# Sets of 128 edges for five destinations in a graph network's adjacency build

## The reference, cut to what matters

```python
x = x + attention(h, qW, kW, vW, src, dst)     # softmax over the edges of a source row
x = x + sage_pool(h, src, dst, ...)            # twice: segment_max(m[src], dst)
x = x + segment_sum((h @ G)[col] * w, row) + bG
x = x + sixteen rounds of  h = 0.9 * segment_sum(norm * h[row], col) + 0.1 * h0
```

## Time and profile before

| | us |
|---|---|
| median of 3 runs | 2932.34 (2927.5 to 2935.43) |
| span of the profiled execution | 2888.9 |
| PE, DVE, ACT, POOL busy | 2545.6, 1856.1, 1190.5, 1187.0 |
| front | 0 to 62.5 |
| build | 62.5 to 249 |
| attention and first dense layer | 249 to 703.6 |
| max pass 1, dense layer, max pass 2 | 703.6 to 1232, to 1311.3, to 1832 |
| third layer, propagation | 1832 to 2090, to 2888.9 |

### The profile page before, as it was taken

One profiled execution on the slowest core, in us unless ns is written; L12 is line 12 of the kernel. 1 busy time (PEld: TensorE's weight loads), 2 busy tenths in 40 slices (PEclk: granted clock), 3 DMA queues, 4 the chain that ended last, 5 costly groups with the idle time before them and its releaser, 6 DMA issues. The chain is left out here.

```text
span 2888.9 us, 69542 instructions
## 1 busy us (share of the span) xinstructions
PE 2545.6 (88%) x27756; PEld 1989.5 (69%) x27756; DVE 1856.1 (64%) x5232; ACT 1190.5 (41%) x2826; POOL 1187.0 (41%) x1385
## 2 busy tenths in 40 slices
PE   5888999995899889756999898368799999999999
PEld 3455777773566566534666565258699999999998
DVE  6997999996788778535887787251244444444444
ACT  4997888884344334423444344231121111111110
POOL 3003999993677667535777677410000000000000
PEclk8999999997999999878999999559999999999999
DMA  5103000004455445423555454529500000000000
GB/s 165 37 1 95 13 12 13 12 11 119 116 136 139 123 126 144 128 76 91 140 146 127 124 144 124 175 73 337 163 2 2 2 2 2 2 2 2 2 2 18
DMA packets 160514, 227.25 MB, mean 79 GB/s; under 512 B 59579, under 2 KB 126454, under 8 KB 159516
## 3 DMA queue, kind: packets, MB, share of 16 engines
q1 hardware_dynamic: 134184, 186.29, 20.8%
q0 software_dynamic: 22464, 35.14, 6.7%
q10 hardware_dynamic: 3540, 1.30, 0.2%
HBM read 122.95 MB, written 102.05 MB: 78 GB/s over the span
## 5 line engine op out<-in xcount | busy, mean ns | idle before, releaser
L1855 POOL DMA_INDIRECT max_row<-table,max_src_rows x640 | 735.1, 1149 | 365.7 <-issue 176.5
L2433 PE MATMUL prop<-g,adj 128*128 128x192 f16 x9216 | 771.1, 246 | 7.1 <-PEq L2104 7.1
L2433 PEld LDWEIGHTS prop<-g,adj 128*128 128x128 f16 x9216 | 760.1, 98 | 14.8 <-issue 12.4
L1737 POOL TENSOR_SCALAR e<-e 128x512 f32<-128x512 f32 (+1 forms) x625 | 365.8, 604 | 219.6 <-ACT e L1725 202.3
L1882 PE MATMUL max_far<-adj 128*96 128x512 f16 x1800 | 428.6, 385 | 4.4 <-issue 4.3
L1751 DVE TENSOR_TENSOR e<-e,a_ps 128x1024 f32<-128x1024 f32 (+1 forms) x313 | 371.4, 1195 | 35.1 <-PE a_ps L1663 13.0
L2522 ACT ACTIVATE g<-prop_state 128x96 f16<-128x96 f32 (+1 forms) x375 | 106.0, 283 | 635.5 <-DVE prop_state L2490 635.5
L1725 ACT ACTIVATE e<-s_ps 128x512 f32<-128x512 f32 (+1 forms) x625 | 335.8, 585 | 61.5 <-PE o_ps L1675 37.1
L1882 PEld LDWEIGHTS max_far<-adj 128*96 128x96 f16 x1800 | 225.4, 125 | 168.5 <-issue 18.6
L1979 DVE TENSOR_TENSOR_SCAN max_run<-max_same,max_run,max_col 96x512 f32<-96x512 f16 x160 | 203.9, 1274 | 210.8 <-issue 190.8
L2488 DVE SCALAR_TENSOR_TENSOR part<-prop,coef,prop_base 128x96 f32<-128x96 f32 x384 | 120.6, 314 | 313.2 <-PE prop L2433 225.8
(11 more groups left out here) (273 smaller groups left out, 3368.4 us busy)
## 6 DMA issues: line engine op xcount, KB each, us to landing
weights<-max_rows_w SPq DMA_DIRECT2D x52, 400.0 KB
rows_dram<-max_out SPq DMA_DIRECT2D x100, 192.0 KB
weights<-adj SPq DMA_DIRECT2D x48, 400.0 KB
ws_w<-weights SPq DMA_DIRECT2D x50, 384.0 KB
max_same<-same_dram SPq DMA_DIRECT2D x196, 96.0 KB
rows_dram<-adj SPq DMA_DIRECT2D x96, 192.0 KB
ws_w<-weights SPq DMA_DIRECT2D x50, 288.0 KB
max_row<-table,max_src_rows POOLq DMA_INDIRECT x640
```

What stands on the lines that cost most here:

```text
L1737: nc.gpsimd.tensor_scalar(e_tile(u), e_tile(u), math.exp(10.0), math.exp(-10.0), ALU.min, ALU.max).then_inc(clipped, 1)
L1855: nc.gpsimd.indirect_dma_start(row[i % RING][:, j, :], None, table_dram, bass.IndirectOffsetOnAxis(ap=src_rows[:, 4 * n + j:4 * n + j + 1] ...
L2433: return nc.tensor.matmul(sums(step, t), adj[:, k, t * P:(t + 1) * P], states[:, k, :], start=start and t % 2 == 0, stop=k == END - 1 and ...
```

## The change

A set is now the 128 edges from the first edge of five destinations (FEW), whatever their number up to 128. A half of 64 destinations has 13 sets (WINS; the last has four destinations), in four steps of 3, 3, 3 and 4 sets, that is 15, 15, 15 and 19 destinations. A key_hot is 125 columns wide, and each set is multiplied into its own columns. 196 steps remain in the build and 100 in a pass; there are 637 sets in the build and 650 in the two passes together, instead of 588 and 600.

In front the windows in DRAM go. Five-destination limits are compared with the first edge of each block of 512; POOL gathers that block's destinations for every set (six gathers of 128 rows), VectorE counts those below the limit (`count_rows(0)` at s = 1, `count_rows(1)` and `find_begins` at s = 2), and POOL gathers 129 joined edges (dst, src, weight) from the found edge on (six gathers). The joined list is made by three copies on POOL and stored by SP. The check for overflow looks at the 129th edge, at s = 5; the scale of the weights follows at s = 6.

```diff
+QUARTER = 4
+HALF = P // 2
+FEW = 5
+FEW_KEYS = FEW * T
+WINS = -(-HALF // FEW)
+STEP_WINS = (3, 3, 3, 4)
+WIN_AT = (0, 3, 6, 9)
...
```

In front, on SP:

```diff
-            sp.wait_ge(pads_made, PADS_TAIL)
-            lists = (dst, src, weight.bitcast(I32))
...
+            sp.wait_ge(rows_joined, 3)
+            by_row = edges_dram.rearrange("(q e) l -> q (e l)", e=BLK)
+            for first_row, last_row in ((0, EVEN_ROWS), (EVEN_ROWS, ROWS)):
+                sp.dma_start(by_row[first_row:last_row, :], joined[first_row:last_row, :, :].rearrange("q e l -> q (e l)")).then_inc(edges_stored, 16)
...
```

In front, on POOL:

```diff
+            for u in range(WT):
+                nc.gpsimd.indirect_dma_start(rows[:, u, :], None, dst.rearrange("(n e) -> n e", e=LINE),
+                                             bass.IndirectOffsetOnAxis(ap=row_i[:, u:u + 1], axis=0)).then_inc(rows_found[u // TURNED], 16)
             pool.wait_ge(rows_loaded, 96)
+            nc.gpsimd.tensor_copy(joined[:, :, 1], src_i[:, :]).then_inc(rows_joined, 1)
+            nc.gpsimd.tensor_copy(joined[:, :, 2].bitcast(F32), w_f[:, :]).then_inc(rows_joined, 1)
+            pool.wait_ge(edges_stored, 32)
+            pool.wait_ge(begin_ready, 1)
+            for u in range(WT):
+                nc.gpsimd.indirect_dma_start(edges[:, u, :, :].rearrange("p e l -> p (e l)"), None, edges_dram,
+                                             bass.IndirectOffsetOnAxis(ap=begin_i[:, u:u + 1], axis=0)).then_inc(gathered[u // TURNED], 16)
...
```

In front, on VectorE:

```diff
+                for u in range(TURNED * v, TURNED * (v + 1)):
+                    last = nc.vector.tensor_scalar(less[:, u, :], rows[:, u, :], bounds[:, 0, u:u + 1], None, ALU.is_lt, ALU.add, accum_out=count[:, u:u + 1])
...
-            for m in range(STARTS):
-                nc.vector.tensor_scalar(below[:, m, :], limit[0:ROWS, :], first[:, m:m + 1], None, ALU.is_gt).then_inc(compared, 1)
+            nc.vector.tensor_scalar(below[:, :], limit[0:ROWS, 0:WT * P], first[:, 0:1], None, ALU.is_gt).then_inc(compared, 1)
...
```

In the build:

```diff
-                for w in range(WIN):
-                    s = WIN * g + w
-                    nc.vector.tensor_scalar(key_hot[:, g % RINGS, w, :], c.iota16[:, :], tables[:, 0, s:s + 1], None, ALU.is_equal).then_inc(hot_ready, 1)
+                for w in range(n):
+                    s = first_win[g] + w
+                    nc.vector.tensor_scalar(key_hot[:, g % RINGS, w, 0:FEW_KEYS], c.iota16[:, 0:FEW_KEYS], tables[:, 0, s:s + 1], None, ALU.is_equal).then_inc(hot_ready, 1)
...
+                    mm = nc.tensor.matmul(count_ps[g % 2][:, FEW_KEYS * w:FEW_KEYS * w + n], lane_hot[:, g % RINGS, w, :], key_hot[:, g % RINGS, w, 0:n], start=True, stop=True)
...
+                nc.scalar.activation(adj[:, :, at:at + n], count_ps[g % 2][:, 0:T * n].rearrange("p (d k) -> p k d", d=n), ACT.Copy).then_inc(kept, 1)
...
```

In a max pass:

```diff
+                    keys_of = key_hot[n % 2][:, w, 0:FEW_KEYS].rearrange("p (k d) -> p k d", k=T)[:, :, 0:m]
...
                     for h in range(2):
-                        mm = nc.tensor.matmul(strip_ps[n % 2][:, 0:KEYS], lane_w[n % 2][:, h, w, :], key_hot[n % 2][:, w, :],
-                                              start=w == 0 and h == 0, stop=w == WIN - 1 and h == 1)
+                        mm = nc.tensor.matmul(by_source(n)[:, :, FEW * w:FEW * w + m], lanes_by_weight(n)[:, h, w, :], keys_of,
+                                              start=w == 0 and h == 0, stop=h == 1, skip_group_check=True)
...
-                nc.scalar.activation(strip_at(0, n), strip_ps[n % 2][:, 0:KEYS].rearrange("p (k d) -> p k d", d=GROUP), ACT.Copy).then_inc(hi_kept, 1)
+                nc.scalar.activation(strip_at(0, n), by_source(n), ACT.Copy).then_inc(hi_kept, 1)
```

More of the change, by code:

```diff
@@ L829, in front @@
         src_t, dst_t, w_t = sb("src_t", [P, CHUNKS], I32), sb("dst_t", [P, CHUNKS], I32), sb("w_t", [P, CHUNKS], F32)
-        first, limit, below = sb("first", [ROWS, STARTS], F32), sb("limit", [P, LIMITS], F16), sb("below", [ROWS, STARTS, LIMITS], F16)
+        first, limit_i, limit = sb("first", [ROWS, 1], F32), sb("limit_i", [P, LIMIT_HALVES * WINS], I32), sb("limit", [P, LIMIT_HALVES * WINS], F32)
+        below, bounds = sb("below", [ROWS, WT * P], F16), sb("bounds", [P, 2, WT], F32)
         zero_rows, far_rows = sb("zero_rows", [PAD_ROWS, P], I32), sb("far_rows", [PAD_ROWS, P], I32)
-        tail = sb("tail", [3, TAIL_SIZE], I32)
-        o_i, o_f, offset = sb("o_i", [P, GT], I32), sb("o_f", [P, GT], F32), sb("offset", [P, GT], F32)
-        begin, end, over = sb("begin", [P, GT], F32), sb("end", [P, GT], F32), sb("over", [P, GT], F32)
+        row_f, row_i, rows = sb("row_f", [P, WT], F32), sb("row_i", [P, WT], I32), sb("rows", [P, WT, BLK], I32)
+        less, count = sb("less", [P, WT, BLK], F16), sb("count", [P, WT], F32)
+        begin, begin_i, offset = sb("begin", [P, WT], F32), sb("begin_i", [P, WT], I32), sb("offset", [P, WT], F32)
+        after, over = sb("after", [P, WT], F32), sb("over", [P, WT], F32)
         any_over, w_scale, first_root = sb("any_over", [P, 1], F32), sb("w_scale", [P, 1], F32), sb("first_root", [P, 1], F32)
-        row_f, row_i = sb("row_f", [P, GT, WIN], F32), sb("row_i", [P, GT, WIN], I32)
-        edges = sb("edges", [P, GT, WIN, 3, P], I32)
-        shape = [P, GT, WIN, P]
+        joined = sb("joined", [ROWS, BLK, 3], I32)
+        edges = sb("edges", [P, WT, P + 1, 3], I32)
+        shape = [P, WT, P]
         lane_i, tile_i = sb("lane_i", shape, I32), sb("tile_i", shape, I32)
@@ L950, in _ @@
+            for v in range(2):
+                lanes(v)
             nc.gpsimd.tensor_copy(src_f[:, :], src_i[:, :]).then_inc(cast, 1)
@@ L978, in values, with turn_table @@
                 mm.then_inc(v_made, 1)
[L980 to L982 removed]
+            def turn_table(table, v, bank, turned):
+                for i in range(TURNED):
+                    mm = nc.tensor.transpose(bank[:, i * P:(i + 1) * P], table[:, TURNED * v + i, :], c.ident[:, :])
                 mm.then_inc(turned, 1)
[L985 to L992 removed]
+            weight_f = edges[:, :, 0:P, 2].bitcast(F32)
+            pe.wait_ge(numbered, 2)
+            for n in range(2):
+                for u in range(WT):
+                    nc.tensor.matmul(bounds_ps[:, n * WT + u:n * WT + u + 1], limit[:, u * P + n:(u + 1) * P + n], c.ident[:, 0:1], start=True, stop=True)
+            pe.wait_ge(compared, 1)
+            for u in range(WT):
+                mm = nc.tensor.matmul(counts[:, u:u + 1], below[:, u * P:(u + 1) * P], c.ones16[0:ROWS, :], start=True, stop=True)
             mm.then_inc(counted, 1)
@@ L1002, in _ @@
                     values(s - 1)
-                if s == 1:
-                    pe.wait_ge(over_kept, 1)
-                    nc.tensor.matmul(over_ps, c.ones[:, :], any_over[:, :], start=True, stop=True).then_inc(over_summed, 1)
                 if s == 5:
@@ L1275, in _ @@
         def _(dve):
-            for g in range(USED_GROUPS):
+            for g in range(STEPS_USED):
                 if g >= RINGS:
                     dve.wait_ge(counted, g - RINGS + 1)
-                t, q, i = g // (2 * QUARTER), g // QUARTER % 2, g % QUARTER
+                half, i = divmod(g, QUARTER)
+                t, q = divmod(half, 2)
                 if g == 0:
@@ L1558, in key_order @@
 def key_order(adj):
[L1560 removed]
+    return buffer_place(adj)[:, 2 * NP - P:2 * NP - P + FEW_KEYS]
 def pooled_parts(adj):
@@ L1781, in max_pass @@
     PARTS = T * QUARTER
-    assert RING == QUARTER and HALF * 2 == P and sum(PIECES) == T and NB <= PARTS <= P
+    WIDEST = max(STEP_WINS)
+    assert RING == QUARTER and sum(PIECES) == T and NB <= PARTS <= P
     with stack() as ctx:
```

320 lines of the change are left out of this document (153 added, 167 removed).

## The result

The changed kernel takes 2917.81 us (median of 20 runs, 2903.34 to 2929.45) where the kernel before, in runs taken with it, takes 2930.19 (20 runs, 2907.84 to 2942.72). The ratio is 0.9959, with a 95% interval of 0.994 to 0.9978: 12.4 us less, 0.4%. The forecast was 68 us less. The direction is right, the size was forecast more than five times too large.

The account below looks back on a forecast made before the run. VectorE was taken to bound the build, three nearly even engines the max passes. Build -15, passes -54 and front +1 made -68 us, so 2932.3 became 2864 us, eight in ten from 2810 to 2925.

Parts of the forecast that it names:

- The base: Whole kernel: profiled span 2888.9 us, timed median 2932.3 us, the 43.4 us between them taken as fixed around the span.
- The build, 15 us: Build of the adjacency: VectorE's key_hot shrinks to 0.16 us, ScalarE becomes the bound, 15 us less (bounds 0 to 18).
- The front, +1: Front: added gathers, counts and stores against removed issues and compares, 1 us more (bounds -3 to +8).
- The passes, 54 us: Two max passes: TensorE's step shrinks from 4.63 to 3.98 us, 54 us less in sum (bounds 20 to 95).
- POOL takes over, and only its own waits can be won: Max passes: POOL needs 4.65 us a step against TensorE's 3.98; 50 us of its waits on max_col are won.
- Rival B: Max passes: gathers shorten too as VectorE's one-source operations shrink, a third of their excess, 40 us more won, 2824 us; chance 0.18.
- Rival C: Unseen costs eat most: build 0, passes -20, front 0, giving 2912 us; chance 0.20.
- Rival D: Max passes: TensorE, idling under POOL, falls to the lower clock; slower, 2963 us at 15% more steps; chance 0.08.
- The sign: Whole kernel: faster by more than 9 us 0.84, within 9 us 0.07, slower 0.09.
- the fallback: Whole kernel: starts if a set of 128 does not hold the edges of five destinations; slower; chance 0.02.

Follow-up runs that it names:

- e7: Changed kernel with the four gathers of a near block in the max passes replaced by plain loads of 128 consecutive rows; ratio 0.8942 to the kernel before.
- e10: Changed kernel with a pause on POOL (a small memset) after each gather of the max passes; ratio 0.997 to the kernel before.
- e16: Changed kernel itself on the lower level, beside the kernel before; 2779.1 us against 2743.5, ratio 1.012.
- e17: Changed kernel with three wide sets of 400 key columns in the max passes, on the lower level; 2729.3 us, ratio 0.9954 to the kernel before.
- e18: Changed kernel with VectorE's scan moved between one-hots and weighting and the far one-hots in the max passes; 2688.4 us against 2739.9 of the kernel before, 0.9818.
- e8: Changed kernel with 24 of 25 far products of a block cut to 128 of 512 columns; ratio 0.9963 to the kernel before.
- e5: Changed kernel itself, run again beside the kernel before on another chip; ratio 0.9968.
- e6: Changed kernel with only two of a block's four gathers issued in the max passes from the fifth near block on; ratio 0.9039 to the kernel before.
- e9: Changed kernel with three of a block's four gathers issued in the max passes from the fifth near block on; ratio 0.9289 to the kernel before.
- e2: Changed kernel with most of the stores of weights left out from the second tile on; 2894.9 us, ratio 1.0028 to the kernel before.
- e3: Changed kernel with ids of far blocks loaded for the first two far blocks only; 2906.5 us, ratio 1.0054 to the kernel before.
- e13: Changed kernel with the second half of three sums left out in the max passes, 12 of some 35 matmuls a step; ratio 1.0241 to the kernel before.
- e14: Changed kernel with each far product of 512 columns issued as two of 256; ratio 1.02 to the kernel before.

## Why the prediction was right or wrong

- **The base.** Wrong: the 43.4 us "around the span" do not exist. The changed kernel's profiled execution ran 2903.34 us with a span of 2901.6, and in every later run the two differ by 1.7 to 1.8. By that the profiled execution of the kernel before took some 2891 us, 40 us under the median of its runs and less than any timed one. The sum was of differences, so this did not move the forecast gain; where those 40 us lay no trace tells.
- **The build, 15 us.** Right, with its working: 16.5 in the profile, between the 15 taken and the 18 of the sum; key_hot 0.162 us where 0.16 was said, four steps 3.34 us on ScalarE where 3.30 was said, ScalarE without a pause. Neither the odd width nor runs of 15 and 19 columns cost anything. That TensorE's granted clock would fall from 0.97 to 0.50, its lower level of 1.2 GHz, in all of the build was not foreseen; it had room, and ScalarE waited for its products only 3.6 us in the whole build.
- **The front, +1.** Within its bounds (-3 to +8): 0.9 us less. The second round of gathers began at 30.44 and VectorE stood 0.42 us at the keys at 38.01, three us earlier than the earlier trace rows had them.
- **The passes, 54 us.** Wrong, and all of the error. TensorE's step did shrink to 4.0 us (e7: 4.04; a strip matmul takes 0.067 us and not 0.056, six in 0.40). The step that failed is the next one: "POOL takes over, and only its own waits can be won", with POOL at 4.65 us a step, a gather at its mean of 1.148 us, and 50 of the 56 us of its waits on max_col gone. On the level where the forecast was measured POOL did not take over: the waits on max_col grew from 34.6 and 32.7 us to 51.4 and 47.6, since TensorE's results came later (57 us became 125 on ScalarE between 740 and 1200 us), and 156 us of pauses on POOL cost nothing (e10). In place of -54 the passes gave about +5 us (the estimate from the medians above). Why the results come late stays open. On the lower level POOL is the bound as the forecast has it, but with wide products already, so that there was no wait to win; and there the fixed price of a gather failed: freeing TensorE took away small waits of VectorE and with them POOL's way in, 1.13 became 1.24 us, and the passes lost 50 us (e16, e17, and e18 as the counter-test).
- **Rival B** had the gathers right and the gain wrong where it was measured: they shortened from 1.138 and 1.159 us to 1.079 and 1.093, 40 us in both passes, just the third of the excess that it named, and POOL spent them waiting. On the lower level it had the right mechanism with the wrong sign. It reckoned how much time VectorE spends in such operations, which fell. What counts there is how long they run without a pause, and that grew.
- **Rival C** named 2912, near the 2918, by a build of nothing and 20 us in the passes; the build gave all and the passes nothing, so that its number was luck. Its "waits that only change their name" comes near to what happened on ScalarE (250 and 251 us).
- **Rival D** did not happen. The granted clock in the passes went from 0.94 and 0.95 to 0.91 and 0.90, and e8, with 0.79 and 0.76 in the passes, took no longer than e5 beside it.
- **The sign.** Slower had 0.09, by the clock, the fallback and a little of C. Faster is what was measured, and the gain lies just beyond the 9 us that the prediction called no change. On the lower level the change is 1.2% slower, by a mechanism that the prediction had only as a gain.

What stays open is why TensorE's results come late on the upper level, and what sets the level. Shown is that it takes gathers (in the steady part of e6 and e7 there is none of it, in e9 some), that fewer columns do not lift it (e8), nor fewer stores or ids (e2, e3), and that POOL can be given 156 us of pauses under it at no cost (e10). Whether the number of matmuls matters was to be told by e13 and e14, and was not.

## What to carry to other kernels

Before a faster engine is counted as a gain, ask which small waits it removes on its neighbours: a wait of 0.15 us on VectorE was a place at which POOL's gathers got through. Do not take the recorded end of a matmul for the moment at which its result lets others go. Price an indirect gather by what VectorE runs while it is issued, not by its mean, and put an operation that leaves the gathers alone, here the scan, between two stretches of one-hots. And repeat the comparison in several groups of runs where a program leans on gathers: the same change was 0.4% faster in some and 1.2% slower in another.

## What was not expected of the hardware

- Two levels for one program: the kernel before takes 2889 to 2930 us in some groups of runs and 2738 to 2744 in others. On the lower no result of TensorE is late, and the difference lies in the stretches with gathers.
- On the upper level, while gathers run, ScalarE waited up to 8.4 us for a release that no recorded end explains; in the step shown above it was 3 to 4 us after the matmul's record, at a granted clock of 1.00.
- A gather that meets one-hots and a weighting without a pause makes almost no way until they end: 3.23 us against 0.94. A plain load that POOL issues among the same one-hots is not held up: 0.546 us (e7).
